# The end of a routed-experts and attention kernel: six of the last block's eight down-projection chunks go down with tokens as columns, and the second copies of the routed rows are added by accumulating transfers on GpSimd's queue

## The reference

```python
xn = _layernorm(x, axis=-1)
x = x + attention(xn) + ffn(xn)

# ffn: routed part
topk_p, topk_i = jax.lax.top_k(probs, K)            # K = 2 experts per token
...
gate = jax.nn.silu(jnp.einsum('ech,ehi->eci', xg, rg))
up = jnp.einsum('ech,ehi->eci', xg, ru)
eout = jnp.einsum('eci,eih->ech', gate * up, rd)
contrib = eout * (w * valid)[..., None]
routed = jnp.zeros_like(xf).at[dispatch.reshape(-1)].add(contrib.reshape(-1, h))
# ffn: shared part
shared = jax.nn.silu(x @ sg) * (x @ su) @ sd
return shared + routed
```

## Time and profile before

| | |
|---|---|
| median of three runs | 159.84 us (159.69 to 160.55) |
| the profiled execution's own time | 160.08 us |
| its span | 158.6 us |
| granted TensorE clock | 1.0 of full in every slice |
| TensorE matmul busy | 96% |
| VectorE busy | 75% |
| ScalarE busy | 66% |
| GpSimd busy | 51% |

### The profile page before, as it was taken

The page is one execution under the profiler, slowest core; times in us unless marked ns, Lnnn a source line. Parts: engine busy times, 40 slices in busy tenths (PEclk is TensorE's granted clock), DMA queues, the critical chain, the costliest instruction groups (busy, mean ns, idle before and its releaser), DMA issues.

```text
span 158.6 us, 3106 instructions
## 1 busy us (share of the span) xinstructions
PE 152.1 (96%) x964; PEld 135.2 (85%) x964; DVE 118.4 (75%) x295; ACT 104.6 (66%) x218; POOL 80.9 (51%) x96
## 2 busy tenths in 40 slices
PE   6989998979999999999999999999999999999992
PEld 6957764978999988888888999999999999878992
DVE  4799959797933789999897777687687686645862
ACT  3359999959876488767866559899686566343200
POOL 7651300357777777877400002698988867354000
PEclk9999999999999999999999999999999999999999
DMA  4999999991111115456069300224142110019486
GB/s 121 267 287 116 172 287 310 342 306 60 55 51 50 50 43 162 109 156 187 12 162 253 130 0 2 102 71 129 35 114 62 50 46 33 29 27 261 110 265 197
DMA packets 26350, 20.72 MB, mean 131 GB/s; under 512 B 2301, under 2 KB 22296, under 8 KB 26336
## 3 DMA queue, kind: packets, MB, share of 16 engines
q1 hardware_dynamic: 24544, 17.89, 43.3%
q0 software_dynamic: 1792, 2.65, 5.3%
HBM read 12.36 MB, written 7.92 MB: 128 GB/s over the span
## 4 chain that ended last, share of the span: by engine, by line
PE 85%; DVE 7%; DMA 3%; SPq 1%; issue 1%; ACT 1%; DVEq 0%; ACTq 0%
PE bank L1147 15%; PE bank L1149 15%; PE bank L1148 15%; PE bank L1228 9%; PE bank L1295 7%; PE bank L1345 5%; PE bank L1347 5%; PE bank L1346 5%; DMA acc<-in_L_attn_x_dram 3%; PE bank L1213 3%; PE bank L1361 2%; PE bank L1372 2%; DVE stats L831 1%; DVE xnT_lo L868 1%; PE bank L1196 1%
## 5 line engine op out<-in xcount | busy, mean ns | idle before, releaser
L648 ACT ACTIVATE silu<-bank 128x512 f32<-128x512 f32 (+1 forms) x64 | 33.2, 521 | 29.6 <-PE bank L1149 29.2
L542 POOL DMA_INDIRECT slots_dram<-row,slot_i x32 | 34.8, 1087 | 12.8 <-issue 9.4
L975 DVE TENSOR_TENSOR bank<-bank,silu 128x320 f32<-128x320 f32 (+1 forms) x48 | 27.2, 566 | 15.7 <-ACT silu L648 12.5
L561 POOL DMA_INDIRECT routed_dram<-eo,xg x24 | 23.0, 957 | 11.6 <-DVE eo L1015 6.3
L981 DVE TENSOR_TENSOR hid_lo<-bank,hid_hi 128x320 fp32r<-128x320 f32 (+1 forms) x48 | 26.3, 548 | 0.0
L1147 PE MATMUL bank<-xnT_hi,sw_hi 128*128 128x512 f32 x62 | 25.4, 410 | 0.4 <-DVE hid_s L975 0.4
L1149 PE MATMUL bank<-xnT_hi,sw_lo 128*128 128x512 f32 x62 | 24.5, 396 | 0.0
L1148 PE MATMUL bank<-xnT_lo,sw_hi 128*128 128x512 f32 x62 | 24.5, 395 | 0.0
L656 ACT CAST hid_hi<-bank 128x320 fp32r<-128x320 f32 (+1 forms) x48 | 22.9, 477 | 0.0
L549 POOL TENSOR_TENSOR ew_lo<-sw_raw,ew_hi 128x1024 fp32r<-128x1024 f32 x3 | 7.2, 2409 | 20.7 <-ACT ew_hi L672 20.7
L1295 PEld LDWEIGHTS bank<-sd,hid_s 128*128 128x128 f32 x128 | 14.9, 192 | 1.0 <-issue 0.9
(11 more groups left out here) (185 smaller groups left out, 312.5 us busy)
## 6 DMA issues: line engine op xcount, KB each, us to landing
sw_raw<-in_L_ffn_rg_dram SPq DMA_DIRECT2D x8, 256.0 KB, 3.1
sw_raw<-in_L_ffn_ru_dram SPq DMA_DIRECT2D x8, 256.0 KB, 3.9
rd_raw<-in_L_ffn_rd_dram SPq DMA_DIRECT2D x8, 256.0 KB, 3.8
routed_dram<-fill SPq DMA_DIRECT2D x1, 2048.0 KB, 12.3
routed<-routed_dram SPq DMA_DIRECT2D x8, 256.0 KB, 4.1
slots_dram<-fill SPq DMA_DIRECT2D x1, 1300.0 KB, 13.6
xg<-slots_dram SPq DMA_DIRECT2D x8, 130.0 KB, 2.4
row<-row SPq DMA_DIRECT2D x1, 1024.0 KB, 8.7
```

The source lines that it names most:

```text
L542: G.indirect_dma_start(slots_dram, bass.IndirectOffsetOnAxis(slot_i[:, k, t:t + 1], 0), row[:, t, 0:RW], None, bounds_check=E * CAP - 1, o ...
L561: G.indirect_dma_start(routed_dram, bass.IndirectOffsetOnAxis(xg[0:n, e % XB, r, 1:2].bitcast(I32), 0), eo[0:n, e % 2, r, :], None, bounds ...
L648: C.activation(silu[:, q % 2, 0:n], gate_bank(q)[:, 0:n], ACT.Silu).then_inc(silu_ready, 1)
L975: V.tensor_tensor(hid, up[:, 0:n], silu[:, q % 2, 0:n], ALU.mult).then_inc(hid_ready, 1)
```

## The change

1. Chunks c0 to c5 of block 3 (`END_WIDE` = 6) join `SPLIT`, and block 3 becomes a last job. They go down as those of blocks 1 and 2 do, through `hid_hi`, `hid_lo`, `sums_b`, `turned_out`. Only c6 and c7 stay in `hid_s`. `down_end_block` is now 4 f32 matmuls for the first half, the four transposes of the wide sum, and 4 for the second half. VectorE adds three pieces to block 3: half, turned sum, half.
2. SyncE loads only the first copies. GpSimd adds the second copies to `acc` by two accumulating transfers (`add_second`): one of 768 KB for blocks 0 to 2 when the first copies of these are added (`summed` at 3), one of 256 KB for block 3 when its first copy is added (`summed` at 4). SyncE's write of blocks 0 to 2 waits for the first of them, VectorE's last three additions for the second.

```diff
+    END_WIDE = CS - 2
+
+    SPLIT = [q for q, (kind, i, c) in enumerate(ORDER)
+             if kind == "expert" or i in WIDE or (i == B - 1 and c < END_WIDE)]
...
-    JOBS = [("block", b) for b in WIDE] + [("expert", e) for e in range(E)]
+    JOBS = [("block", b) for b in WIDE] + [("expert", e) for e in range(E)] + [("block", B - 1)]
+    LAST_EXPERT = JOBS.index(("expert", E - 1))
...
-        return CLOSE if q == END else min(q + LAG, END + 1)
+        if q == END:
+            return CLOSE
+        return min(q + LAG, END + 1 if q < END else len(ORDER) - 1)
...
+        end_banks = [turn_b[0], gate_bank(at["block", B - 1, CS - 2])]
...
-            load_routed(0)
-            sp.wait_ge(eo_written[1], 48 * (E // 2))
-            load_routed(1)
+            load_routed()
+            sp.wait_ge(second_added[0], 16)
             for g in range(B - 1):
-                sp.wait_ge(summed, B + g + 1)
                 sp.dma_start(out_v[g], acc[:, TG * g:TG * g + TG, :]).then_inc(out_written, 16)
             for h in range(2):
-                sp.wait_ge(block_added, B + h)
+                sp.wait_ge(block_added, B + 1 + h)
...
+            def add_second(i, first, last):
+
+                pool.wait_ge(summed, last)
+                G.dma_start(acc[:, TG * first:TG * last, :].rearrange("p t d -> p (t d)"),
+                            routed_v[1, :, first:last, :].rearrange("p b e -> p (b e)"), accum_op=ALU.add
+                            ).then_inc(second_added[i], 16)
+
+            for i in range(2):
+                pool.wait_ge(eo_written[i], 48 * (E // 2))
+            add_second(0, 0, B - 1)
+            add_second(1, B - 1, B)
...
+            copy_out(len(JOBS) - 1)
...
                 elif kind == "block" and i == B - 1 and c >= CS - 3:
-                    add_routed(0, c - (CS - 3))
-            add_routed(0, B - 1)
-            dve.wait_ge(summed, B)
-            for g in range(B):
-                add_routed(1, g)
-            dve.wait_ge(summed, 2 * B)
+                    add_routed(c - (CS - 3))
+            add_routed(B - 1)
+            dve.wait_ge(second_added[1], 16)
             end_block_sum(0)
+            dve.wait_ge(block_added, B)
+            block_sum(B - 1)
+            dve.wait_ge(block_added, B + 1)
             end_block_sum(1)
...
-                b = B - 1
-                first, second = turn_b[0], sums_b
+                b, cs = B - 1, range(END_WIDE, CS)
                 pe.wait_ge(xg_ready, E)
-                pe.wait_ge(hid_ready, at["block", b, CS - 2])
-                down_tile(first[:, 0:D], 0, range(CS - 2))
-                pe.wait_ge(out_copied, len(JOBS))
-                down_tile(second[:, 0:D], 2, range(CS - 2))
                 pe.wait_ge(hid_ready, at["block", b, CS - 1] + 1)
-                down_tile(first[:, 0:D], 0, range(CS - 2, CS))
-                down_tile(first[:, D:2 * D], 1).then_inc(end_down, 1)
-                down_tile(second[:, 0:D], 2, range(CS - 2, CS))
-                down_tile(second[:, D:2 * D], 3).then_inc(end_down, 1)
+                for h in range(2):
+                    if h == 1:
+                        turn_out(len(JOBS) - 1)
+                    for r in range(2):
+                        last = down_tile(end_banks[h][:, D * r:D * r + D], 2 * h + r, cs, END_WIDE)
+                    last.then_inc(end_down, 1)
```

More of the change, by code:

```diff
@@ L86, in closing_chunk @@
         kind, i = job
-        return at[kind, i, (CS if kind == "block" else CR) - 1]
+        chunks = CR if kind == "expert" else CS if i in WIDE else END_WIDE
+        return at[kind, i, chunks - 1]
     def job_after(step):
-        for n, job in enumerate(JOBS[:-1]):
+        for n, job in enumerate(JOBS[:LAST_EXPERT]):
             if down_step(closing_chunk(job)) + 1 == step:
@@ L109, in moe_attention_kernel @@
     out_v = out.rearrange("b (t p) d -> b p t d", p=P)
-    routed_v = routed_dram.rearrange("(k p b t) d -> k b p (t d)", k=2, b=B, p=P)
+    routed_v = routed_dram.rearrange("(k p b t) d -> k p b (t d)", k=2, b=B, p=P)
     with ExitStack() as ctx:
@@ L244, in moe_attention_kernel @@
         with ExitStack() as room:
-            routed = room.enter_context(nc.sbuf_tensor("routed", [P, 2, NT, D], F32))
+            routed = room.enter_context(nc.sbuf_tensor("routed", [P, NT, D], F32))
         bank = [ctx.enter_context(nc.psum_tensor(f"bank{i}", [P, 512], F32)) for i in range(8)]
@@ L296, in moe_attention_kernel @@
         eo_written = [sem(f"eo_written{i}") for i in range(2)]
-        routed_loaded = [[sem(f"routed_loaded{k}{g}") for g in range(B)] for k in range(2)]
+        routed_loaded = [sem(f"routed_loaded{g}") for g in range(B)]
+        second_added = [sem(f"second_added{i}") for i in range(2)]
         row2_copied = sem("row2_copied")
@@ L419, in next_slots, with load_routed @@
                 load_slots(e)
-            def load_routed(k):
+            def load_routed():
                 for g in range(B):
-                    sp.dma_start(routed[:, k, TG * g:TG * g + TG, :].rearrange("p t d -> p (t d)"), routed_v[k, g]
-                                 ).then_inc(routed_loaded[k][g], 16)
+                    sp.dma_start(routed[:, TG * g:TG * g + TG, :].rearrange("p t d -> p (t d)"), routed_v[0, :, g, :]
+                                 ).then_inc(routed_loaded[g], 16)
             for e in range(2, 5):
@@ L760, in _ @@
                 if q == CLOSE:
-                    copy_out(len(JOBS) - 1)
+                    copy_out(LAST_EXPERT)
                 if q - 1 in nth_split:
@@ L1022, in end_block_sum, with add_routed @@
                 a = acc[:, t:t + 2, :].rearrange("p t d -> p (t d)")
-                V.tensor_tensor(a, (turn_b[0], sums_b)[h][:, 0:2 * D], a, ALU.add).then_inc(block_added, 1)
-            def add_routed(k, g):
+                V.tensor_tensor(a, end_banks[h][:, 0:2 * D], a, ALU.add).then_inc(block_added, 1)
+            def add_routed(g):
                 if g < B - 1:
                     dve.wait_ge(block_added, g + 1)
-                dve.wait_ge(routed_loaded[k][g], 16)
+                dve.wait_ge(routed_loaded[g], 16)
                 ts = slice(TG * g, TG * g + TG)
-                V.tensor_tensor(acc[:, ts, :], routed[:, k, ts, :], acc[:, ts, :], ALU.add).then_inc(summed, 1)
+                V.tensor_tensor(acc[:, ts, :], routed[:, ts, :], acc[:, ts, :], ALU.add).then_inc(summed, 1)
             stats_of(0)
@@ L1290, in up_of_block, with down_tile @@
                          xnT_hi[:, S * b:S * b + S], xnT_lo[:, S * b:S * b + S], between)
-            def down_tile(o, i, cs=range(CS)):
+            def down_tile(o, i, cs=range(CS), first=0):
                 for c in cs:
                     last = M(o, hid_s[:, c, P * i:P * i + P], sd[:, c, :],
-                             start=(c == 0), stop=(c == CS - 1))
+                             start=(c == first), stop=(c == CS - 1))
                 return last
@@ L1333, in down_chunk @@
                 if kind == "block":
-                    w_hi, w_lo, close = sd_hi[:, c, :], sd_lo[:, c, :], c == CS - 1
+                    w_hi, w_lo, close = sd_hi[:, c, :], sd_lo[:, c, :], q == closing_chunk((kind, i))
                     pe.wait_ge(sd_split, 1)
@@ L1430, in _ @@
                 if q == CLOSE:
-                    turn_out(len(JOBS) - 1)
+                    turn_out(LAST_EXPERT)
                 elif job_after(q) is not None:
```

1 line of the change is left out of this document (removed).

## The result

The changed kernel takes 167.92 us (median of four runs, 167.53 to 168.17), the kernel before, timed beside it, 160.05 us. The ratio is 1.0487 with a 95% interval of 1.0449 to 1.0525: slower by 7.9 us. The forecast was 167.0 us in a range of 163.5 to 171.0. The profiled execution took 168.03 us with a span of 166.1. In eight of the twelve runs of the experiments (e1 to e4 and e9 to e12) the attention stage took 32 to 37 us longer in every kernel, the one before included, whose medians beside them were 197.0 and 192.09 us (in the profile of e1 TensorE ran no matmul between 60 and 77 us); the cause stays open, and their totals say little about the end of the program.

A forecast was written before the change was run, and what follows sets the result against it. TensorE's matmuls and the second copies both run into the end, the copies slightly ahead. Landing 161.3 + 1.7 + 0.2 + 2.53 = 165.7 us of span, + 1.48 - 0.24 = 167.0 us; range 163.5 to 171.0.

The forecast's parts named there:

- What bounds the end: End of the program: second copies land last; TensorE, done at 154.90, is hidden by over 3 us, its 0.73 us worth nothing.
- The chunks in between: Block 3: c0 to c3 going down between chunks end the last up matmul 2.80 us later, at 151.27; ScalarE and VectorE fit.
- The start of the transfers: GpSimd's queue: issues at 153.44 and 154.71, 0.77 us after VectorE's addition, 0.97 us each, 0.30 us between.
- The price of an accumulating transfer: Second copies into `acc`: one and a half times a plain transfer; 768 KB land at 159.8, 256 KB at 161.3.
- plain price: Second copies: 1.05 MB at 265 GB/s, 3.96 us; as a rival, the add is free, 164.8 us, chance 0.22.
- the sum's own 1.9 us ahead of the data: First transfer's start: 2.15 us, from a 64 KB indirect write, less 0.25 us for its data.
- the half-rate rival: Accumulating transfers: two reads through one port, twice the plain price; span 167.9, time 169.2 us, chance 0.22.
- the forecast's own sign: 768 KB after their issue starts: in place sooner than 4.9 us means plain price, later than 7.5 half rate or worse.
- A dear issue: GpSimd's issue: descriptors written slowly or rows cut, 2 us or more on top of either rate; 169 to 172 us, chance 0.09.
- What stands behind the landing: After the 256 KB land: VectorE's three additions 1.7 us, 0.2 for output beside them, then last output transfer 2.53 us.
- The 0.2 us that the sum added: End of the program: allowance for the 0.79 MB output of blocks 0 to 2 meeting the last accumulate for about half a microsecond.
- Beside the span: Time outside the span: 1.48 us, less 0.24 for the profiled execution over the median, added to 165.7 us.

The follow-up runs named there:

- e1: Item 1 of the change only, second copies loaded by SyncE and added by VectorE as before: ratio 1.0016 to the kernel before, stage 1.40 us longer.
- e4: Changed kernel with the two transfers issued by SyncE as plain copies that overwrite `acc`: ratio 1.0176 to the kernel before, stage 25.59 us.
- e9: Item 1, plain loads, first copies added one chunk earlier, GpSimd adding block 0's second copy: ratio 1.0134 to the kernel before, stage 22.53 us.
- e12: Second run of the changed kernel with GpSimd's two transfers as plain copies that overwrite `acc`: ratio 1.0241 to the kernel before, stage 26.53 us.
- the eight runs named above: Changed kernel, its plain-copy runs (GpSimd twice, SyncE once), item 2 only (twice), TensorE's tail longer, first copies earlier: landing of 768 KB to end 5.44 to 5.51 us.
- e3: Changed kernel with GpSimd's two transfers as plain copies that overwrite `acc`, first run: ratio 1.0225 to the kernel before, stage 26.38 us.
- the run with two blocks: Item 1, plain loads, first copies added one chunk earlier, GpSimd adding second copies of blocks 0 and 1: ratio 1.0078 to the kernel before.
- e2: Item 2 only: the kernel before with the accumulating transfers, first run: ratio 1.023 to the kernel before, stage 25.83 us.
- e7: Changed kernel with second copies added onto loaded first copies in `routed`, four transfers, VectorE adding each block once: 164.17 us, ratio 1.0262 to the kernel before.
- e11: Item 2 only, run again: the kernel before with the accumulating transfers: ratio 1.0273 to the kernel before, stage 25.95 us.
- part 1 alone: Item 1 of the change only, second copies loaded and added as before, run twice: ratios 1.0016 and 1.0138 to the kernel before.

## Why the prediction was right, point by point

- **What bounds the end.** Right. The time hangs on the second copies; TensorE ended at 155.08 (forecast 154.90), and 2.7 us more of it cost nothing.
- **The chunks in between.** Right. The last up matmul ended at 151.49 against 151.27, in a stage that began 0.23 us later. ScalarE and VectorE stayed beside TensorE: their longer pauses in the stage wait for TensorE.
- **The start of the transfers.** Right: issues at 153.49 and 154.14 against 153.44 and 154.71. GpSimd starts 0.62 us after the addition and not 0.77. The second issue follows without the 0.30 us pause, while the first still counts as busy.
- **The price of an accumulating transfer.** The term that was mis-sized, twice, in opposite directions. The sum had one and a half times a plain price of 265 GB/s, 5.9 us. With the sum's own 1.9 us ahead of the data, measured are 6.5 us, as 1.9 times a plain price of 306 GB/s. That factor is the half-rate rival's. "Collectives: The Full Stack" of the Trainium skill (section "The bandwidth ceiling: the fold count and why AG ≠ RS ≠ AR") gives a measured ratio of 1.93 for a reduce-scatter against an all-gather, whose add needs two source reads; the 1.9 of these runs agrees with it, though it hangs on the 1.9 us that are taken off, and the whole times give 1.6. The plain price was too dear. The 265 comes from a stretch in which scatters shared the engines, which may be why; that was not tested. The measured 306 lies between it and the 342 of the best slice. The forecast also held that the trace speaks against a rate above 342, and in one microsecond the plain copies moved 434. The landings at 160.6 and 161.9, against 159.8 and 161.3, were near because the two errors cancel, which is luck. By the forecast's own sign, 4.9 us for a plain price and 7.5 for half rate, the 7.1 us of the 768 KB lie between the two.
- **A dear issue.** No: the issues counted 1.0 to 1.3 us busy, in a direct form with 6 KB or 2 KB a partition, against 0.97 for the indirect one. Nothing of it grew with the bytes. Against the 0.57 to 0.60 us of a plain direct issue it is dearer, though, and the data start 0.4 us later; the two microseconds of the rival did not come.
- **What stands behind the landing.** VectorE's three additions took 1.61 us (1.7) and the rest of the span 2.58 (2.53), so the sum fits. But the path was the wrong one, or at least not the only one. The forecast said that SyncE's queue would be free when block 3 is ready. The queue is, the DMA engines are not: in the eight runs named above the output takes 5.44 to 5.51 us from the landing of the 768 KB, wherever VectorE's last addition lies. 160.63 + 5.47 and 163.52 + 2.58 both give 166.1 here, so this miss cost nothing; with plain copies it was 0.6 us. The 0.2 us that the sum added for the output beside the last transfer can't be told apart.
- **Beside the span.** The sum took 1.48 us for what lies outside it, and it was 1.93. About half of the 0.9 us between 167.0 and 167.92 is this, the other half the span (165.7 against 166.1).

Where the 7.3 us of the stage come from, by the runs: 4.3 for the accumulating transfers where they would have started before, 2.8 because part 1 starts them later, and the rest of 0.2 is not resolved. Of the 4.3 some 2.3 to 2.5 are the add itself with its longer issue (e3 and e12 against the changed kernel), 0.8 to 0.9 GpSimd's queue, both taken from the changed kernel's stage. About 1 us is left, and no run takes it apart. The transfers wait for VectorE where SyncE's loads waited only for expert 7, and the output of blocks 0 to 2 waits for all three; that these make up the rest is argued, not shown.

## What to carry to other kernels

A transfer that adds into a live tile has to wait until the tile's other writers are done, and so it moves from the slack in the middle to the end of the chain; ask first when the last writer ends, and only then how long the transfer takes. Its bytes moved at about half the plain rate here, and from first issue to last landing it took 1.6 times as long. Count also what waits for its landing, the output's bytes above all. And take a gain on one engine for nothing until the engine that is next (VectorE here, 0.57 us behind) has been counted with the instructions that the change adds to it.

## What the runs showed of the hardware

- Accumulating transfers from DRAM into SBUF moved 184 to 209 GB/s at a DMA share of 1.0, plain ones of the same shape 319 to 363 at a share of 0.87 to 0.89 in one run, and 434 at 1.07 in the fullest microsecond of the other.
- An addition with both operands in SBUF on GpSimd's engine and one on VectorE disturb each other: VectorE's took 1.5 to 1.65 us instead of 0.68, GpSimd's 1.75 instead of 1.29 where VectorE had begun first and 1.28 where it had not. c7's product, which reads one operand from PSUM, ran wholly beside an addition of GpSimd in the run with two blocks (151.16 to 151.85) and took its usual 0.69.
- The granted TensorE clock fell from 1.0 to 0.50 (the level of 2.4 and that of 1.2 GHz) at about 159.5, with TensorE without work since 155.08. No matmul was left to pay for it. The time outside the span was 1.7 to 2.0 us in the executions of the changed kernel and of e2 to e7, e11 and e12, and 1.4 to 1.55 in those of the kernel before and of part 1 alone. A low clock at the end does not go with it: the profiles of e1 and e9 end at 0.50 too, with 1.47 and 1.55 us outside the span. The run with two blocks shows both, 1.47 to 1.51 in three executions and 1.72 to 1.78 in the other three. What makes the difference stays open.
